# Layer norm of x for four batches at once, its Newton steps on GpSimd between the probabilities' low halves

## The reference, cut to what matters

```python
def _layernorm(x, axis=-1, eps=1e-05):
    m = jnp.mean(x, axis=axis, keepdims=True)
    v = jnp.var(x, axis=axis, keepdims=True)
    return (x - m) / jnp.sqrt(v + eps)
...
    x = x + jnp.tanh(g_xattn[0]) * _L0_xattn_ref(_layernorm(x, axis=-1), ctx_768, mask_BxS2_bf1, ...)
    x = x + jnp.tanh(g_ffn[0]) * _L0_ffn_ref(_layernorm(x, axis=-1), ...)
```

## Time and profile before

| | |
|---|---|
| time, median of 3 runs | 1670.24 us (1670.09 to 1671.91) |
| the profiled execution | 1668.12 us, its span 1666.3 us |
| mean granted TensorE clock | 0.98 of full speed |
| busy share of PE, DVE, ACT, POOL | 91%, 89%, 56%, 40% |
| DMA, mean | 71 GB/s |

### The profile page before, as it was taken

How to read it: one execution, slowest core, us unless ns; L and a number is a source line. 1 busy time by engine, 2 the same in 40 slices (tenths; PEclk the granted TensorE clock), 3 DMA queues, 4 the chain that set the end, 5 groups by cost and what they waited for, 6 DMA issues and landing times.

```text
span 1666.3 us, 48258 instructions
## 1 busy us (share of the span) xinstructions
PE 1511.3 (91%) x14501; PEld 1010.6 (61%) x14501; DVE 1487.7 (89%) x4375; ACT 938.2 (56%) x1799; POOL 668.6 (40%) x813
## 2 busy tenths in 40 slices
PE   3899999999999999999999999997999999999998
PEld 2566666666666666666666666664666666666665
DVE  7799999999999999999999999987888888888886
ACT  2465656565656666566656565644555554555554
POOL 5355555455554545554555555452111111111111
PEclk9799999999999999999999999986999999999999
DMA  2333333333333333333333333311010110101101
GB/s 79 89 97 85 94 85 86 97 86 97 83 96 83 97 84 93 87 89 92 86 97 83 98 81 97 80 47 55 27 38 25 38 36 27 38 25 38 38 25 51
DMA packets 207471, 117.93 MB, mean 71 GB/s; under 512 B 24912, under 2 KB 207184, under 8 KB 207440
## 3 DMA queue, kind: packets, MB, share of 16 engines
q1 hardware_dynamic: 207440, 117.54, 26.1%
HBM read 32.53 MB, written 16.78 MB: 30 GB/s over the span
## 4 chain that ended last, share of the span: by engine, by line
PE 54%; DVE 26%; issue 13%; ACT 4%; DVEq 2%; DMA 0%; ACTq 0%
PE bank L1060 12%; PE bank L308 9%; PE bank L1090 5%; PE bank L1089 5%; DVE smax L745 5%; PE bank L332 4%; PE bank L315 4%; PE bank L299 4%; DVE xres L790 3%; DVE rstd L685 3%; DVE k L715 2%; DVE rstd L687 2%; PE bank L387 2%; DVE y L1047 2%; DVE rstd L678 2%
## 5 line engine op out<-in xcount | busy, mean ns | idle before, releaser
L915 POOL TENSOR_TENSOR probl<-prob 128x512 f16<-128x512 f32 x512 | 528.9, 1041 | 535.8 <-ACT prob L597 534.9
L597 ACT ACTIVATE prob<-bank,masks 128x512 f32<-128x512 f32 x512 | 345.2, 687 | 144.9 <-PE bank L367 144.9
L745 DVE TENSOR_REDUCE smax<-bank 128x4 f32<-128x512 f32 x512 | 348.1, 681 | 14.5 <-PE bank L332 10.6
L1076 DVE TENSOR_TENSOR hidl<-hid 128x512 f16<-128x512 f32 x256 | 226.9, 886 | 79.5 <-ACT hid L1071 78.8
L1071 ACT ACTIVATE hid<-bank,b_sb 128x512 f32<-128x512 f32 x256 | 175.9, 687 | 212.3 <-PE bank L1060 206.1
L1060 PE MATMUL bank<-y,w1T 128*128 128x512 f16 x1024 | 262.9, 379 | 29.9 <-DVE y L1047 28.4
L1154 POOL TENSOR_TENSOR xres<-xres,b2g 128x1024 f32 (+1 forms) x32 | 75.7, 2365 | 431.3 <-ACT yln L1024 413.4
L1089 PE MATMUL bank<-w2T,hid 128*128 128x256 f16 x1024 | 237.4, 273 | 1.4 <-ACT w2T L1004 1.4
L1090 PE MATMUL bank<-w2T,hidl 128*128 128x256 f16 x1024 | 237.3, 273 | 0.0
L332 PE MATMUL bank<-k_rows,q_rows 34*128 34x128 f16 x2048 | 228.0, 222 | 6.8 <-DMA q_rows<-smaxT 3.4
L367 PE MATMUL bank<-q_rows,k_rows 50*128 50x128 f16 x2048 | 204.4, 221 | 0.9 <-DMA q_rows<-smaxT 0.9
(11 more groups left out here) (90 smaller groups left out, 2555.7 us busy)
## 6 DMA issues: line engine op xcount, KB each, us to landing
q_rows<-q SPq DMA_DIRECT2D x512, 64.0 KB, 2.6
k_rows<-k SPq DMA_DIRECT2D x512, 64.0 KB, 2.5
xres<-in_x_dram SPq DMA_DIRECT2D x64, 256.0 KB, 2.7
out_dram<-ystage SPq DMA_DIRECT2D x32, 512.0 KB, 2.9
ctx_sb<-in_ctx_dram SPq DMA_DIRECT2D x64, 192.0 KB, 3.1
q_rows<-smaxT SPq DMA_DIRECT2D x128, 8.0 KB
w_raw<-in_L_ffn_W_dram SPq DMA_DIRECT2D x2, 1024.0 KB, 6.7
prob<-in_L_xattn_Wq_dram SPq DMA_DIRECT2D x1, 256.0 KB, 3.9
```

The lines of the kernel that those rows point to most:

```text
L597: act.activation(prob[u][:], st_bank[u % 2][:], ACT.Exp, bias=0.0, scale=masks[g.parity][:, 2 + b:3 + b]).then_inc(exp_done, 1)
L745: dve.tensor_reduce(smax[:, b, u * UH:(u + 1) * UH], sm_bank[u % 2][:].rearrange("p (h j) -> p h j", h=UH), AX.X, ALU.max).then_inc(max_ta ...
L915: pool.tensor_tensor(probl[u][:], prob[u][:], prob[u][:].bitcast(BF16)[:, 1::2], ALU.subtract).then_inc(prob_split, 1)
```

## The change

- Attention's norm goes by halves of four batches (an iteration of the loop) instead of by groups of two: tiles of 128x4, once for two groups. Results are in a tile of their own, `norm`.
- From the third half on, DVE does only the seed (`seed_x`, four parts: `bn_stats`, aggregation, variance, seed) in even groups, at `norm(0)` to `norm(3)`; `norm(0)` now stands ahead of the group's first `take_max`. Odd groups have no part of the norm on DVE.
- The Newton rounds become 14 multiplications and additions on GpSimd (`root_x`), two behind each `low_prob` of an even group but the first; each waits for the one before it. The last raises `ln_ready`.
- `load_x` takes four batches (512 KB), in odd groups only, behind a wait for `ln_ready`.
- The first two halves are normed by DVE as before, four batches at a time, in the stretch ahead of the loop.
- In `ln_part` the product with -0.5 moves from part 3 to part 2, and the last product goes to `norm`; `norm_y` begins with part 0 at `norm(0)`.

```diff
-LN_AHEAD = 8
+SEED_PARTS = 4
+ROOT_PARTS = 2 + 4 * NEWTON
...
-        rstd = sb("rstd", [P, 4, QB], F32)
+        rstd = sb("rstd", [P, 3, QB], F32)
+        norm = sb("norm", [P, 2, QB], F32)
+        newton = sb("newton", [P, 5, QB], F32)
+        minus1, one5 = sb("minus1", [P, QB], F32), sb("one5", [P, QB], F32)
...
-        def load_x(sp, g):
-            sp.dma_start(xres[:, bass.ds(g.batch(0), 2), :], x_v[:, bass.ds(g.batch(0), 2), :]).then_inc(
-                x_in[g.parity], 16)
+        def load_x(sp, half):
+            sp.dma_start(xres[:, bass.ds(half * QB, QB), :], x_v[:, bass.ds(half * QB, QB), :]).then_inc(x_in, 16)
...
-            x_past = held(2 * (g.n + 3))
-            if left >= 4:
-
-                sp.wait_ge(ln_done, x_past)
-                load_x(sp, g.after(4))
+            x_past = held(g.half + 3) if g.parity == 1 else None
+            if g.parity == 1 and left >= 6:
+
+                sp.wait_ge(ln_ready, x_past)
+                load_x(sp, g.half + 3)
...
+        def seed_x(dve, half, i):
+
+
+            past = half - 2
+            if i == 0:
+                dve.wait_ge(x_in, 16 * (half + 1))
+                for b in range(QB):
+                    last = dve.bn_stats(stats[:, b, :], row_of(half * QB + b))
+            elif i == 1:
+
+                if not (isinstance(half, int) and half == 2):
+                    dve.wait_ge(ln_ready, half)
+                dve.wait_ge(seed_step, past * (SEED_PARTS - 1) + 1)
+                dve.tensor_copy(rstd[:, 2, :], stats[:, :, 1])
+                for b in range(QB):
+                    last = dve.bn_aggr(meanvar[:, b, :], stats[:, b, :])
+            elif i == 2:
+                dve.wait_ge(seed_step, past * (SEED_PARTS - 1) + 2)
+                dve.tensor_scalar(newton[:, 2, :], meanvar[:, :, 1], EPS, -0.5, ALU.add, ALU.mult)
+                last = dve.tensor_scalar(newton[:, 0, :], meanvar[:, :, 1], EPS, None, ALU.add)
+            else:
+                dve.wait_ge(seed_step, past * (SEED_PARTS - 1) + 3)
+                dve.tensor_scalar(newton[:, 1, :].bitcast(I32), newton[:, 0, :].bitcast(I32), -0.5, RSQRT_SEED,
+                                  ALU.mult, ALU.add).then_inc(root_seeded, 1)
+                return
+            last.then_inc(seed_step, 1)
+
+        def root_x(pool, half, i):
+
+
+            y, hv, t, mean = (newton[:, k, :] for k in range(1, 5))
+            past = half - 2
+            if i == 0:
+                pool.wait_ge(root_seeded, past + 1)
+                pool.wait_ge(root_step, past * (ROOT_PARTS - 1) + 1)
+                last = pool.tensor_tensor(mean, meanvar[:, :, 0], minus1[:], ALU.mult)
+            else:
+                pool.wait_ge(root_step, past * (ROOT_PARTS - 1) + (i + 1))
+                if i == ROOT_PARTS - 1:
+                    pool.tensor_tensor(norm[:, 1, :], norm[:, 0, :], mean, ALU.mult).then_inc(ln_ready, 1)
+                    return
+                if i == ROOT_PARTS - 2:
+
+                    pool.wait_ge(ln_done, QB * half)
+                    last = pool.tensor_tensor(norm[:, 0, :], y, t, ALU.mult)
+                elif i % 4 == 1:
+                    last = pool.tensor_tensor(t, y, y, ALU.mult)
+                elif i % 4 == 2:
+                    last = pool.tensor_tensor(t, t, hv, ALU.mult)
+                elif i % 4 == 3:
+                    last = pool.tensor_tensor(t, t, one5[:], ALU.add)
+                else:
+                    last = pool.tensor_tensor(y, y, t, ALU.mult)
+            last.then_inc(root_step, 1)
...
             def norm(i):
                 if left == 0:
 
-                    norm_y(dve, Group(0, 0), ((i - LN_AHEAD) % LN_PARTS,))
-                if i < LN_AHEAD and left >= 4:
-                    norm_x(dve, g4, (i,))
-                if i >= LN_AHEAD and left >= 3:
-                    norm_x(dve, g3, (i,))
-
-
+                    norm_y(dve, Group(0, 0), (i,))
+                if g.parity == 0 and left >= 4 and i < SEED_PARTS:
+                    seed_x(dve, g.half + 2, i)
+
+            norm(0)
             take_max(dve, g, 1, 2)
-            norm(8)
             if not first:
                 add_attention(dve, g.batch(0) - 2)
-            norm(9)
+            norm(1)
             take_max(dve, g, 1, 3)
             round_max(dve, g, 1)
-            norm(10)
+            norm(2)
             low_max(dve, g, 1)
+            norm(3)
             if not first:
                 read_weighed(dve, g.batch(0) - 1, 1, 1)
                 normalise(dve, g.batch(0) - 1, 1, 1)
...
                     low_prob(pool, g, b, u)
+                    k = b * UNITS + u
+                    if g.parity == 0 and left >= 4 and k >= 1:
+                        for i in range(2 * k - 2, 2 * k):
+                            root_x(pool, g.half + 2, i)
                     if b == 1 and u == 0 and left >= 1:
                         pick_masks(pool, g.after(1))
```

More of the change, by code:

```diff
@@ L169, in bass_gated_cross_attention_ternary_ffn @@
         gates_set = sem("gates_set")
-        x_in = [sem(f"x_in{p}") for p in range(2)]
+        x_in = sem("x_in")
         ctx_loaded = [sem(f"ctx_loaded{p}") for p in range(2)]
@@ L526, in apply_x @@
         def apply_x(act, g):
-            act.wait_ge(ln_ready, g.n + 1)
+            act.wait_ge(ln_ready, g.half + 1)
             if not (isinstance(g.half, int) and g.n == 0):
@@ L531, in apply_x @@
             for b in range(2):
-                act.activation(xln[:, b, :], row_of(g.batch(b)), ACT.Identity, bias=rstd[:, 3, b:b + 1],
-                               scale=rstd[:, 1, b:b + 1]).then_inc(ln_done, 1)
+                r = 2 * g.parity + b
+                act.activation(xln[:, b, :], row_of(g.batch(b)), ACT.Identity, bias=norm[:, 1, r:r + 1],
+                               scale=norm[:, 0, r:r + 1]).then_inc(ln_done, 1)
         def copy_xT(act, g):
@@ L658, in ln_part @@
         def ln_part(dve, i, rows, step, base, ready):
-            n = len(rows)
-            half, y, t, shift = (rstd[:, k, 0:n] for k in range(4))
+            half, y, t = (rstd[:, k, :] for k in range(3))
             if i > 0:
@@ L688, in ln_part @@
             else:
-                last = dve.scalar_tensor_tensor(y, t, 1.5, y, ALU.add, ALU.mult)
+                last = dve.scalar_tensor_tensor(norm[:, 0, :] if i == LN_PARTS - 2 else y, t, 1.5, y, ALU.add,
+                                                ALU.mult)
             last.then_inc(step, 1)
@@ L693, in row_of, with norm_x @@
             return xres[:, bass.ds(batch, 1), :].rearrange("p o d -> p (o d)")
-        def norm_x(dve, g, parts):
+        def norm_x(dve, half, parts):
             for i in parts:
                 if i == 0:
[L698 to L703, removed]
+                    dve.wait_ge(x_in, 16 * (half + 1))
+                if i == LN_PARTS - 2 and not (isinstance(half, int) and half == 0):
+                    dve.wait_ge(ln_done, QB * half)
+                rows = [row_of(half * QB + b) for b in range(QB)] if i == 0 else ()
+                ln_part(dve, i, rows, ln_step, half * (LN_PARTS - 1), ln_ready)
@@ L816, in dve_first @@
             dve.wait_ge(mask_set, 1)
-            norm_x(dve, g1, range(LN_PARTS))
             low_q(dve, g0)
@@ L821, in dve_first @@
             low_k(dve, g0)
-            norm_x(dve, g0.after(2), range(0, LN_AHEAD))
+            norm_x(dve, 1, range(0, LN_PARTS - 2))
             low_v(dve, g0)
-            norm_x(dve, g0.after(2), range(LN_AHEAD, LN_PARTS))
+            norm_x(dve, 1, range(LN_PARTS - 2, LN_PARTS))
             low_q(dve, g1)
@@ L878, in dve_group @@
                 low_k(dve, g2)
+            norm(8)
             if not first:
                 add_attention(dve, g.batch(0) - 1)
+            norm(9)
             if left >= 1:
@@ L1011, in norm_y @@
             for i in parts:
-                if i == 3 and not (isinstance(g.half, int) and g.n == 0):
-                    dve.wait_ge(y_done, QB * g.n)
-                rows = [row_of(g.n * QB + b) for b in range(QB)] if i == 0 else (None,) * QB
+                if i == LN_PARTS - 2:
+                    if isinstance(g.half, int) and g.n == 0:
+                        dve.wait_ge(ln_done, B)
+                    else:
+                        dve.wait_ge(y_done, QB * g.n)
+                rows = [row_of(g.n * QB + b) for b in range(QB)] if i == 0 else ()
                 ln_part(dve, i, rows, y_step, g.n * (LN_PARTS - 1), y_ready)
@@ L1023, in apply_y @@
             for b in batches:
-                act.activation(yln[:, b, :], row_of(g.n * QB + b), ACT.Identity, bias=rstd[:, 3, b:b + 1],
-                               scale=rstd[:, 1, b:b + 1]).then_inc(y_done, 1)
+                act.activation(yln[:, b, :], row_of(g.n * QB + b), ACT.Identity, bias=norm[:, 1, b:b + 1],
+                               scale=norm[:, 0, b:b + 1]).then_inc(y_done, 1)
         def transpose_y(pe, g):
```

55 lines of the change are left out of this document (26 added, 29 removed).

## The result

The changed kernel takes 1718.11 us (median; 1705.09 to 1732.62) against 1670.16 us (1667.74 to 1671.91) for the kernel before beside it: a ratio of 1.0267, 95% interval 1.0198 to 1.0336. The prediction was 1665 us with a range of 1650 to 1684 and "faster" at 0.48. It is wrong: the time lies above the range and far above the 1680 of its slow rival. The runs of the new kernel spread by 1.6%, those of the old one by 0.25%.

A forecast was written before the change was run, and what follows sets the result against it. PE and DVE were both near full, with DVE's order at group heads on the path. A pair came to 22.0 + 11.7 = 33.7 against 33.92 us, taken as -0.17; over 28 pairs -5, so 1665 us, range 1650 to 1684.

The forecast's parts named there:

- slow rival: GpSimd's steps end later and delay PE through SP undiminished: a loss from 0.3 us a pair, 1680 at 0.7; chance 0.28.
- the restart: From PE's odd rough scores to the next even context transposes: 11.96 before, 11.7 us forecast.
- DVE's heads: DVE's work before each group's context transposes: odd head 1.98 to 1.13 us, even head 2.46 to 2.55.
- Even to odd: Even to odd context transposes: 14.38 + 1.13 = 15.51 us, a gain of 1.57.
- The even head with its statistics: DVE before even context transposes, with four `bn_stats`: 2.55 us against 2.46, so +0.09.
- if nothing else held: A pair of groups with only DVE's head changes counted: 32.44 us, less 1.48.
- full-gain rival: SP's wait is hidden and the whole head gained: 29 pairs of 1.4 us, -41, so 1629 us; chance 0.12.
- The mechanism at SP: SP's load of x waits for `ln_ready`, delaying `move_max` to 19.95; PE stands 1.6 us at odd `scores`.
- The first term: GpSimd's last norm step, counted from the even context transposes: done at 13.6 us; the load leaves 0.05 later.
- The second: DVE's chain after odd rough scores starts 0.3 to 0.45 us earlier: 0.35 of the wait returned.
- -0.17: Net change taken per pair: 33.7 against 33.92 us is -0.2, trimmed for DVE and GpSimd meeting.
- DVE's share of 80%: Sign of being right: DVE's share of the span near 80%, having lost 132 us of busy time.

The follow-up runs named there:

- the early load: Changed kernel, but SP's load of x in odd groups waits for the seed instead of the last GpSimd step: 1623.2 us, ratio 0.9723.
- half dose: Changed kernel, but SP's load of x in odd groups waits for the even group's last low half instead of the last GpSimd step: 1669.25 us, ratio 1.0007.
- late load: Kernel before, but SP's load of x in odd groups also waits for the group's second exponential: 1811.76 us, ratio 1.0866.
- the steps on DVE: Kernel with the early load, but the Newton steps back on DVE, for four batches at once, none on GpSimd: 1745.09 us, ratio 1.0451.

## Why the prediction was wrong

The step that failed is PE's wait for `move_max` and what comes behind it: the wait and the restart were mis-sized by 0.7 us a pair, and that TensorE's clock falls behind the wait was put at nothing.

*DVE's heads were right.* Even to odd: 15.51 worked out, 15.60 measured. The even head with its statistics, 2.55 worked out:

```profile
638.17 1.40 DVE L716 BATCH_NORM_STATS2 stats<-xres 128x6 f32 x4
639.48 0.68 DVE L804 TENSOR_REDUCE smax<-bank 128x4 f32<-128x512 f32 x1
640.07 0.48 DVE L849 SCALAR_TENSOR_TENSOR xres<-bank,gates,xres 128x256 f32 x1
```

L292 at 640.68 is 2.51 behind the first of them. The 32.44 a pair that I wrote "if nothing else held" is the 32.47 of the early load; its 1623 us are the full-gain rival's 1629.

*The mechanism at SP was right, and mis-sized in two terms.* All from the even L292:

| term | predicted | changed kernel | half dose |
|---|---|---|---|
| last GpSimd step done | 13.6 | 13.81 | |
| load of x leaves | 13.65 | 14.02 | 13.66 |
| `move_max` leaves | 19.95 | 20.38 | 19.97 |
| PE starts the odd L336 | 22.0 | 22.47 | 22.01 |
| from there to the next L292 | 11.7 | 11.97 | 11.96 |
| pair | 33.7 | 34.44 | 33.97 |

The first term: GpSimd's chain ended 0.2 late (0.28 between dependent steps, a step at 0.25, low halves at 1.10 and 1.11 beside DVE), and SP's load left 0.21 behind the end of the last step where I had 0.05. The second: I credited the wait with 0.35 returned, since DVE's chain to the transposes of x starts earlier. It does: L282 is 2.44 behind L336 (2.96 in the earlier trace rows). But DVE's two-input `low_max` (L819) now falls beside a low half on GpSimd, takes 0.91 and gave it back, so that PE stood 0.55 at L350; at the same place in the kernel with the early load it takes 0.17:

```profile
631.77 1.04 POOL L969 TENSOR_TENSOR probl<-prob 128x512 f16<-128x512 f32 x1
...
631.93 0.91 DVE L819 SCALAR_TENSOR_TENSOR smax<-smax 128x16 f16<-128x16 f32 x1
```

```profile
636.23 0.17 DVE L819 SCALAR_TENSOR_TENSOR smax<-smax 128x16 f16<-128x16 f32 x1
```

From L336 to L292 the time was 11.96 to 11.99 in this kernel, the one before, the early load and the half dose. Together 0.7 us a pair: +0.5 instead of -0.17, near the point at which the slow rival decides, though its cause (the steps) carries 0.2 of it. This is 19 of the 53 us between forecast and time. (By the prediction's own sum 0.7 us in each of 28 pairs gives 1665 + 20 = 1685 us, not the 1680 that it wrote; with the clock held up the changed kernel took 1685.27.)

*The term that was missing is the larger one.* "The new one PE would be there at 20.39 and stands 1.6 us" was costed as 1.6 us. The step took each standstill at its own length, with TensorE's speed afterwards unchanged. The granted clock fell to 1.2 GHz behind it in two odd groups of three, for part or all of the rest: 33 us in the median run and 42 in the profiled one against the kernel with two extra matmuls, 49 over the 28 pairs of the trace. Filling the gap removes it in three kernels (the changed one, the one before with a late load, the one with the steps on DVE), nothing else being earlier; so it is PE's standing still there, and not the new work, that lowers the clock. The Trainium skill, "TensorE: Matmul & The Clock Gate", section "HAM oscillation — how this bites in real kernels", describes waits between bursts of matmuls that are paid for a second time by the clock, again in every round of a loop. The runs here agree, though in the changed kernel only 19 of 28 rounds paid. It was a rival that I should have priced.

*The signs.* The gap of about 3 us on SP and `move_max` directly behind the moves came as said. DVE's share of 80% did so by luck: it lost 110 us where I had 132, and 1378 us would have been 83% of the span that I forecast. Odd to even at full clock was 18.8 where I said 18.1. The standstill was 1.28 us on the mean where I said 1.6, and the profile puts it down to "issue", not to the transfer.

What stays open: why the clock fell in two thirds of the odd groups of the changed kernel, in all those of the loop with the late load in the kernel before, and in three of four even groups with the steps on DVE. There the standstill that the filler removed, 0.89, is that of the half dose, where the clock hardly fell. The second gap of 0.33 is a difference; with the first one filled it alone did no harm. Nor is the length alone what decides: in the kernel with the early load PE stands 1.16 us before every even L292, longer than in either of those, and the clock never falls behind it. What makes the standstill at one place harmful and at another not, no run here separates.

## What to carry to other kernels

A wait put into an in-order queue is priced by what stands behind it there, not by the transfer that it guards: the same wait cost 95 us ahead of `move_max` (1718.11 against 1623.2) and nothing that can be told behind it (1624.31). A standstill of TensorE in a loop costs more than its length where the clock falls behind it, and it does not fall behind every one: look at the granted clock of the stretch after it, first try to move the wait, and where that can't be done give PE something to do. And where a sum of large terms comes out near zero, the restart terms decide its sign; take them from a row (11.96 was there to be read) before crediting anything back.

## What was not expected of the hardware

- Extra matmuls whose results are thrown away made kernels faster: by 33 us (two in each odd group of the changed kernel) and by 91 us (two in each even group with the steps on DVE), the mean granted clock rising from 0.918 to 0.981 in the second.
- Equal standstills did not have equal effects: after one of 1.26 us odd to even took 18.80, after the next one, of 1.27 us, 22.16, in one execution of one kernel. Yet this need not be chance. In the kernel before with the late load, with standstills of 1.40 to 1.47 us, odd to even comes back in the same order every six pairs (twice 23.6 to 23.7, then 20.1, 19.9, 19.7 and 22.4); with the steps on DVE every third or fourth even group is spared. When a standstill comes seems to matter as well as how long it is; to what its time is tied, no run here shows. The changed kernel's time spreads from 1705 to 1733 us, while the one with the steps on DVE, whose clock falls just as often, keeps within 9 us.
- A matmul of 128x256 f32 as filler appears twice in the records and takes 0.5 us: four (x8) took 1.99.
